# Moving the loads of the token staging ring from GpSimd's queue to SyncE's, in a decoder layer with a mixture of experts

## The reference: what is computed

```
logits = h @ w_router                      # 2048 tokens, 8 experts
top_w, top_i = top_k(softmax(logits), 2)
y = silu(h @ w_gate_e) * (h @ w_up_e) @ w_down_e      # per expert, inner width 352
routed = sum over the two chosen experts, weighted by top_w
sh = silu(h @ w_sh_gate) * (h @ w_sh_up) @ w_sh_down  # shared expert, inner width 1408
x = x + routed + sh * sigmoid(h @ w_sh_eg)
```

## Time and profile before

| | us |
|---|---|
| median of 3 runs | 2553.44 |
| lowest and highest | 2552.82 and 2558.96 |
| profiled execution | 2558.96 |
| its span in the profile | 2557.2 |
| PE busy | 2399.1 (94% of the span) |
| DVE, ACT and POOL busy | 1353.7, 1348.8 and 919.3 |

### The profile page before, as it was taken

How to read it: one execution, slowest core, us unless ns; L and a number is a source line. 1 busy time by engine, 2 the same in 40 slices (tenths; PEclk the granted TensorE clock), 3 DMA queues, 4 the chain that set the end, 5 groups by cost and what they waited for, 6 DMA issues and landing times. The chain is left out here.

```text
span 2557.2 us, 39125 instructions
## 1 busy us (share of the span) xinstructions
PE 2399.1 (94%) x15376; PEld 1547.3 (61%) x15376; DVE 1353.7 (53%) x2114; ACT 1348.8 (53%) x1708; POOL 919.3 (36%) x608
## 2 busy tenths in 40 slices
PE   7997899989999999999997999998899999999997
PEld 5885644444444444444333555555578899999885
DVE  5566634434344434434413556555475577776785
ACT  4221467666767777767895434433332266665221
POOL 1223744655355544655202333332034012121320
PEclk8998999999999999999999999999899999999999
DMA  5002675576547653775653300001045267775430
GB/s 181 17 1 72 192 224 126 126 197 170 141 116 209 168 153 93 180 203 143 173 124 104 111 1 1 18 18 53 34 140 170 90 228 233 243 244 186 152 113 37
DMA packets 206983, 331.46 MB, mean 130 GB/s; under 512 B 71312, under 2 KB 125840, under 8 KB 206608
## 3 DMA queue, kind: packets, MB, share of 16 engines
q1 hardware_dynamic: 188304, 252.80, 34.9%
q0 software_dynamic: 16336, 72.23, 8.6%
q10 hardware_dynamic: 2160, 3.93, 0.6%
HBM read 241.53 MB, written 99.42 MB: 133 GB/s over the span
## 5 line engine op out<-in xcount | busy, mean ns | idle before, releaser
L938 ACT ACTIVATE A_c_prob<-c_psum 128x1024 f32<-128x1024 f32 x832 | 787.1, 1029 | 285.9 <-PE c_psum L1188 273.0
L864 POOL TENSOR_TENSOR c_rr<-c_ms,c_half 128x32 f32<-128x32 f32 (+1 forms) x72 | 372.6, 5177 | 426.4 <-DVE c_ms L955 424.8
L1197 PE MATMUL c_psum<-A_c_prob,c_vq 128*17 128x512 f32 x3328 | 417.0, 601 | 8.3 <-DVE c_oT L1092 8.1
L134 PE MATMUL c_psum<-R_c_w,S_c_c 128*128 128x512 f32 x1248 | 313.9, 401 | 0.7 <-DVE S_c_c L966 0.5
L1188 PE MATMUL c_psum<-c_qq,c_kq 64*128 64x512 f32 x1664 | 288.3, 438 | 26.6 <-DMA c_vq<-vd 14.5
L134 PEld LDWEIGHTS c_psum<-R_c_w,S_c_c 128*128 128x128 f32 x1248 | 227.9, 189 | 121.9 <-issue 40.7
L1188 PEld LDWEIGHTS c_psum<-c_qq,c_kq 64*128 64x128 f32 x1664 | 136.9, 186 | 175.6 <-ACT A_c_prob L938 92.6
L995 DVE COPY Q_c_unit<-c_psum 128x256 f32<-128x256 f32 x89 | 37.8, 425 | 333.6 <-PE c_psum L134 333.6
L2363 PE MATMUL m_psum<-A_m_dn_hi,A_m_a 128*128 128x512 f32 (+1 forms) x628 | 204.4, 394 | 2.4 <-DVE A_m_a L2160 2.4
L134 PE MATMUL m_psum<-R_m_t,m_up_hi 128*128 128x256 f32 (+1 forms) x1104 | 200.0, 283 | 0.0
L1616 DVE TENSOR_REDUCE s_topx<-s_psum 128x4 f32<-128x2048 f32 (+1 forms) x64 | 95.5, 1493 | 172.2 <-PE s_psum L1719 167.5
(11 more groups left out here) (298 smaller groups left out, 4282.1 us busy)
## 6 DMA issues: line engine op xcount, KB each, us to landing
c_kq<-kd SPq DMA_DIRECT2D x248, 208.0 KB, 6.1
kd<-S_c_t SPq DMA_DIRECT2D x96, 256.0 KB
Q_c_raw<-in_ctxT SPq DMA_DIRECT2D x89, 256.0 KB
qd<-A_c_q SPq DMA_DIRECT2D x64, 256.0 KB
c_qq<-qd SPq DMA_DIRECT2D x64, 256.0 KB, 3.1
vd<-A_c_vt SPq DMA_DIRECT2D x104, 136.0 KB, 4.1
c_vq<-vd SPq DMA_DIRECT2D x31, 442.0 KB, 9.1
R_m_hs<-slots SPq DMA_DIRECT2D x23, 512.0 KB
```

What stands on the lines that cost most here:

```text
L134: mm = pe.matmul(out, a(c), b(c), start=first and i == 0, stop=last and i == len(terms) - 1)
L864: pool.tensor_tensor(rr[:, unit % RB, 0:n], ms[:, unit % RB, 0:n], half[:, 0:n], ALU.pow).then_inc(s_r, 1)
L938: act.activation(prob[:, t % PB, 2 * (u % 2):2 * (u % 2) + 2, :], score_banks[u % 3], ACT.Exp, scale=XD ** -0.5).then_inc(s_ex, 1)
L1197: mm = pe.matmul(o_bank[32 * j:32 * j + VW, :], vq[:, q % 2, kt, j, :], prob[:, t % PB, j, :], start=kt == 0, stop=kt == CT - 1)
```

## The change

POOL issues no ring load any more; it waits for a tile (`s_ring`) and scatters it. SP issues all sixteen, in three pieces between its weight loads: tiles 0 and 1 before the down weights of unit 1, tiles 2 to 7 behind the down weights of unit 2, tiles 8 to 15 behind those of unit 3. The wait for a free ring buffer goes with each load.

```diff
+            def load_ring(qs):
+                for q in qs:
+                    if q >= RINGS:
+                        sp.wait_ge(s_scat[q % RINGS], 16 * 2 * (q // RINGS))
+                    sp.dma_start(ring[q % RINGS], hx[q * P:(q + 1) * P]).then_inc(s_ring[q % RINGS], 16)
+
             load_down(0)
-            for w in range(1, UNITS):
+            for j in range(2):
+                load_half(1, j)
+            load_ring(range(0, RINGS))
+            load_down(1)
+            for j in range(2):
+                load_half(2, j)
+            load_down(2)
+            load_ring(range(RINGS, NTILE // 2))
+            for j in range(2):
+                load_half(3, j)
+            load_down(3)
+            load_ring(range(NTILE // 2, NTILE))
+            for w in range(4, UNITS):
                 for j in range(2):
                     load_half(w, j)
                 load_down(w)
@@ gpsimd
-            def load_ring(q):
-                if q >= RINGS:
-                    pool.wait_ge(s_scat[q % RINGS], 16 * 2 * (q // RINGS))
-                pool.dma_start(ring[q % RINGS], hx[q * P:(q + 1) * P]).then_inc(s_ring[q % RINGS], 16)
-
-            load_ring(0)
             pool.wait_ge(s_slot, 1)
             for q in range(NTILE):
-                if q + 1 < NTILE:
-                    load_ring(q + 1)
                 pool.wait_ge(s_ring[q % RINGS], 16 * (q // RINGS + 1))
```

## The result

The changed kernel takes 2577.86 us (median of 4 runs, 2576.88 to 2579.58) against 2554.39 us of the kernel before beside it (4 runs, 2552.82 to 2558.96). The ratio is 1.0093, 95% interval 1.0081 to 1.0105: 23.5 us slower, inside the stated range, 8 us over the forecast of 2570. All seventeen executions of it on record lie between 2572.49 and 2582.86 us.

The account below looks back on a forecast made before the run. PE was taken as the bound, so waits added to it count in full. Two waits and the slow clock behind each, 9.6 + 2.9 + 3.3 + 0.7 = 16.5 us on the median 2553.44, gave 2570 us, range 2559 to 2583.

Parts of the forecast that it names:

- What bounds the kernel: PE, busy for 94% of the span; any wait added to it reaches the end in full, other waits being 2.4 us.
- What is removed is worth nothing: Sixteen issues of 0.58 us and buffer waits leave POOL; its chain may end some us earlier, counted as zero.
- Head of the queue: On SP, ring loads waiting for scatters hold back unit 3's halves by 19 us, against 4.0 us of slack.
- First wait: PE at the down product of pass 4 waits 9.6 us because unit 3's halves land late.
- The 4.7: Microseconds assumed for a half load on SP to land after its issue; ends 4.3 and 7.0.
- Second wait: PE at the down product of pass 6 waits 3.3 us for what follows unit 4's late halves.
- the row of 4.3: Trace figure: 4.3 us from a tile's first scatter to the next ring load, when both scatters have landed.
- The clock: PE runs at 1.2 GHz behind its waits at passes 4 and 6, costing 2.9 and 0.7 us.
- The coupling: The wait at pass 4 makes PE late, so what it loses the wait at pass 6 has less.
- The waits were not covered: Concerns the rival that slack covers the waits at pass 4's down product: no measurable change, 2553 us; chance 0.10.
- the second rival: Scatters land late beside SP's loads, 4.5 us more for each of five, 23 us more, 2592 us; chance 0.07.
- Signs: Expected in the trace: late half loads on SP, ACT waiting about 15 us, POOL idle about 1888 to 1907 us.

Follow-up runs that it names:

- the first block only: Changed kernel with ring loads 2 to 7 still ahead of unit 3's halves, but unit 4's halves ahead of ring loads 8 to 15: 2564.18 us, ratio 1.0046.
- six buffers unpaced: Changed kernel with six ring buffers instead of two, SP's order as in the change, POOL scattering without added waits: 2560.15 us, ratio 1.0021.
- both pairs of halves first: Changed kernel with unit 3's halves ahead of ring loads 2 to 7 and unit 4's ahead of 8 to 15: 2552.23 us, ratio 0.9998.
- the two waits on SP: Kernel before, no transfer moved; SP waits for tile 5's scatters ahead of unit 3's halves, tile 13's ahead of unit 4's: 2570.05 us, ratio 1.0066.
- the second block only: Changed kernel with unit 3's halves ahead of ring loads 2 to 7, but ring loads 8 to 15 still ahead of unit 4's halves: 2573.10 us, ratio 1.0070.
- six buffers and the halves first: Changed kernel with six ring buffers, unpaced scatters, and the halves of units 3 and 4 ahead of the ring loads: 2562.32 us, ratio 1.0026.

## Why the prediction was right, and where its sizes were off

- *What bounds the kernel.* Right. PE's waits grew by 19.4 us, and the end moved by these and the slow clock. Nothing behind gave any of it back.
- *What is removed is worth nothing.* Right: POOL's chain ended 2 us earlier to no effect. I had expected some 6; the ring's turns on SP were longer than assumed.
- *Head of the queue.* Right in place and mechanism, shown by the two experiments that move the wait without the transfers and the transfers without the wait.
- *First wait, forecast 9.6 us, measured 11.8.* Set against the first pass's start, the halves went out 0.7 us later than worked out, took 5.8 us until ACT read them instead of 4.7, and the chain over ACT and DVE took 11.0 instead of 10.5, because ACT waited another 0.6 us for the second half. The 4.7 was a median over 20 transfers of the whole run; right behind a ring load and beside scatters it was the wrong row, and the 5.5 of the earlier trace rows would have been nearer.
- *Second wait, forecast 3.3 us, measured 7.6.* This is the mis-sized term. The halves of unit 4 inherit the first round's 2.2 us, and from ring load 8 to ring load 15 the ring took 28.5 us (1932.50 to 1960.99) instead of 26.1. Most of these 2.4 us are one late step: the scatters of tile 9 had landed only 6.2 us after their start, where the row of 4.3 was used, and the two turns behind that took 7.7 and 7.8 us instead of 7.4. Its two rows are shown below. Elsewhere this step took 4.0 to 5.1 us, and a tile 2.8 to 3.6 us from its issue to its first scatter (one 4.3), against the 3.1 taken. Landing and chain add 0.7. The wait ends 5.3 us later than forecast, while PE, whose first slow stretch was shorter, came only 1.0 us later than assumed.
- *The clock, forecast 2.9 and 0.7 us, measured 1.5 and 2.4.* Right in sum (3.6 against 3.9), by luck: in the kernel with the first block only, the same wait of 11.81 us at the same product is followed by 6.2 us of slow clock, not 2.9. Nor does a wait near 2.23 us always cost nothing, as the forecast had it (see the last section).
- *The coupling.* "What the first wait loses the second has less" is borne out by the two blocks alone: 33 us against 23.5. The end of the kernel follows the end of the second wait. What the forecast lacks, 23.3 less 16.5 us, is therefore the 5.3 us by which this wait ended later and the 1.7 us by which the slow stretch behind it cost more, 7.0 by rounded figures.
- *Rivals.* The waits were not covered. The late scatters of the second rival came once and smaller, 1.9 us for tile 9 instead of 4.5 us for each of five.
- *Signs.* The halves of unit 3 near 1922 and of unit 4 near 1961, with the 4.4 us between the frames 1917.5 and 1957: measured 1918.1 and 1961.4. ACT's wait was 16.8 us where about 15 were given, and POOL was idle for 19.8 us with tile 2 missing, where 19 were. The last scatter, given as 1966, that is 1961.6 in the new frame, went out at 1965.6.
- *Slips in the working.* The last scatter's end and landing take 3.0 us by its own row (4.3 less the 1.3 to the second scatter), not 2.7, and 6.4 us at a clock of 0.52 lose 3.1 us, not 3.2. Neither changes the forecast.

The late step of the second round, from the first scatter of tile 9 to the next load of its buffer:

```profile
1939.37 0.96 POOL L2016 DMA_INDIRECT slots<-A_m_spare,m_slot  x1 [0.30 <-issue]
...
1945.55 0.32 SPq L1953 DMA_DIRECT2D A_m_spare<-hx  x1
```

## What to carry to other kernels

A queue that issues DMAs is an engine in its own right: before a transfer is moved onto it, look at what stands behind it in its order and how much slack each of those has, not at how busy the queue is. A transfer whose wait is already met was nearly free here (two tiles, ratio 0.9992); one that waits for another engine holds up everything behind it and costs what exceeds the slack there, so put transfers with a deadline ahead of transfers with a wait. And when two delays follow each other on one path, work out when the second would end, not how long it lasts: alone they cost 12 and 21 us here, together 23.5.

## What the runs showed of the hardware

- DVE was idle for 5.9 to 9.4 us ahead of its second multiplication (1.5 us in the kernel before) and ACT for 6.4 to 10.9 us ahead of the high part that follows it (2.0 to 3.0 us), with nothing in the trace that explains it, in all three kernels in which POOL scattered tile after tile every 2.5 us and the DMA engines were busy for 0.84 to 0.89 of the 24 us around it; not in the one where each tile waited for the scatters of the one ahead (0.50). The cause stays open. With six buffers unpaced the ten runs spread over 12.7 us, those of the kernel before beside them over 6.9; that it is the pause that varies isn't shown.
- PE's clock behind a pause isn't told by the pause's length. Behind every pause of 3.62 to 17.34 us in this part, and behind the one of 3.30 in the earlier trace rows, it was 1.2 GHz; behind 2.99 and 3.12 us it was 2.4 GHz. But the pause of 2.24 us at one of the last down products, the same in all thirteen kernels, left it at 2.4 GHz in nine profiled executions and was followed by 1.2 GHz in four: with both pairs of halves first (first matmul 0.80 us at 2536.85, then a granted clock of 0.50 for 3 us), with the two waits on SP, with the second block only and with six buffers and the halves first.
- Nor does the longer pause make the longer slow stretch: 2.9 us behind 11.78 us, 6.2 behind 11.81, 4.8 behind 7.59, 3.0 behind 4.52.
